# Pair stage: the second-layer products of two rounds issued in one stretch

## What is computed

```python
h = jnp.einsum('bsd,fd->bsf', xn, W1)                                   # 128 features
pair = jax.nn.relu(h[:, :, None, :] - h[:, None, :, :] + b1)
pair = jax.nn.relu(jnp.einsum('bijf,gf->bijg', pair, W2) + b2)          # first product, 128 -> 64
sim = jnp.einsum('bijg,og->bijo', pair, W3)[..., 0] + b3[0]             # second product, 64 -> 1
sim = sim.at[:, diag, diag].set(0.0)
_, top_idx = jax.lax.top_k(sim, 51)
```

## Time and profile before

| | |
|---|---|
| median of 3 runs | 3355.33 us (3354.02 to 3365.64) |
| the profiled execution | 3371.59 us, span 3370.1 us |
| pair stage in the span | 43.7 to 1131 us |
| attention a after it, to | about 1690 us |
| feed-forward, attention b, feed-forward | the rest |
| mean granted TensorE clock | 0.963 of full speed |
| PE / DVE / ACT busy over the span | 93% / 63% / 45% |

### The profile page before, as it was taken

How to read it: one execution, slowest core, us unless ns; L and a number is a source line. 1 busy time by engine, 2 the same in 40 slices (tenths; PEclk the granted TensorE clock), 3 DMA queues, 4 the chain that set the end, 5 groups by cost and what they waited for, 6 DMA issues and landing times.

```text
span 3370.1 us, 44081 instructions
## 1 busy us (share of the span) xinstructions
PE 3147.4 (93%) x17024; PEld 1740.1 (52%) x17041; DVE 2132.8 (63%) x4098; ACT 1518.2 (45%) x2512; POOL 572.6 (17%) x423
## 2 busy tenths in 40 slices
PE   6999999999999799999889999987898987999999
PEld 2333333333333344444268888853444434888887
DVE  5887988888888777667154434444766765443443
ACT  4877877777787356666521111112433442111110
POOL 0000000000000533343010100002543551001100
PEclk9999999999999799999889999988999998999999
DMA  2000000000000000000010100014323311000001
GB/s 70 1 1 11 1 1 11 1 1 11 1 1 1 1 1 1 2 1 1 1 75 19 38 19 1 1 61 115 93 65 88 97 36 75 19 19 19 19 1 50
DMA packets 32245, 86.94 MB, mean 26 GB/s; under 512 B 7139, under 2 KB 7140, under 8 KB 29605
## 3 DMA queue, kind: packets, MB, share of 16 engines
q1 hardware_dynamic: 29702, 83.96, 8.4%
q10 hardware_dynamic: 2336, 0.17, 0.0%
HBM read 59.60 MB, written 20.97 MB: 24 GB/s over the span
## 4 chain that ended last, share of the span: by engine, by line
PE 40%; DVE 3%; POOL 2%; issue 2%; DMA 2%; ACT 1%; SPq 0%; POOLq 0%; DVEq 0%; ACTq 0%
PE ps L1113 21%; PE ps L1127 10%; PE ps L1472 3%; POOL ex_sum L1440 2%; PE ps L1536 2%; PE ps L1503 1%; PE ps L1460 1%; PE ps L1514 1%; PE ps L1488 1%; DMA k_stack<-halves 1%; DMA halves<-lo_b 0%; PE ps L1525 0%; DMA ffn_raw<-in_w_ffn 0%; PE ps L1095 0%; DVE ffn_z L1139 0%
## 5 line engine op out<-in xcount | busy, mean ns | idle before, releaser
L626 DVE TENSOR_SCALAR pair_in<-key_words,row_words 128x512 f32<-128x512 f32 x1792 | 727.0, 480 | 75.9 <-PE ps L513 72.9
L711 ACT ACTIVATE pair_mid<-ps,row_bias 128x512 f32<-128x512 f32 x896 | 573.6, 686 | 236.9 <-PE ps L513 192.4
L513 PE MATMUL ps<-pair_in,w_hi 128*64 128x512 f16 x3584 | 610.4, 393 | 26.5 <-DVE pair_in L626 25.5
L1191 ACT ACTIVATE ffn_silu<-ps 128x512 f32<-128x512 f32 x128 | 76.4, 597 | 829.6 <-PE ps L1113 829.6
L1154 DVE TENSOR_TENSOR ffn_inner<-ffn_silu,ps 128x512 f32<-128x512 f32 x128 | 87.9, 687 | 566.5 <-PE ps L1113 566.5
L513 PEld LDWEIGHTS ps<-pair_in,w_hi 128*64 128x64 f16 x3584 | 204.5, 108 | 403.5 <-ACT pair_mid L711 189.1
L923 DVE TENSOR_REDUCE maxes<-ps 128x2 f32<-128x1024 f32 x256 | 307.8, 1224 | 129.5 <-PE ps L858 127.0
L966 ACT ACTIVATE ex<-ps 128x512 f32<-128x512 f32 x512 | 294.1, 597 | 149.1 <-PE ps L877 132.5
L513 PE MATMUL ps<-pair_in,w_lo 128*64 128x512 f16 x1792 | 354.0, 389 | 0.0
L1113 PE MATMUL ps<-ffn_z_hi,ffn_w_hi 128*128 128x512 f32 x1024 | 276.9, 392 | 7.6 <-DVE ffn_z_lo L1146 7.6
L1113 PE MATMUL ps<-ffn_z_lo,ffn_w_hi 128*128 128x512 f32 x1024 | 276.2, 392 | 0.0
(11 more groups left out here) (190 smaller groups left out, 4164.1 us busy)
## 6 DMA issues: line engine op xcount, KB each, us to landing
ffn_raw<-in_w_ffn SPq DMA_DIRECT2D x16, 1536.0 KB, 6.7
q_stack<-halves SPq DMA_DIRECT2D x48, 256.0 KB, 5.1
k_stack<-halves SPq DMA_DIRECT2D x48, 256.0 KB, 5.9
halves<-hi_b SPq DMA_DIRECT2D x16, 512.0 KB, 2.6
halves<-lo_b SPq DMA_DIRECT2D x16, 512.0 KB, 3.6
x<-in_x SPq DMA_DIRECT2D x8, 512.0 KB, 5.5
out<-x SPq DMA_DIRECT2D x4, 1024.0 KB, 4.3
wb_qk<-in_wb_qk SPq DMA_DIRECT2D x1, 2048.0 KB, 8.3
```

Of the source, the lines that this page charges most:

```text
L513: s = nc.tensor.matmul(ps[F2 * half:F2 * half + F2, bank + which, :], w_part[:, :], words.rearrange("p (s two) -> p s two", two=2)[:, :, o ...
L626: s = nc.vector.tensor_scalar(p.pair_in[:, (4 * n + i) % N_PAIR, :], p.key_words[:, b % 2, :], p.row_words[:, b % 2, row:row + 1], None, A ...
L711: nc.scalar.activation(p.pair_mid[:, n % NG, which, :], ps[:, bank + which, :], ACT.Relu, bias=bias).then_inc(p.mid_made, 1)
```

## The change

`layer2` steps are collected: the list `behind` takes every round, and only behind `pair` of an odd round are all the collected ones issued, those of the round two back and of the round before. Behind `pair` of an even round nothing is issued. `sim` of a tile comes with `layer2` of its round 15, so it now stands behind `pair` and `act_row` of round 1 of the next tile, and is followed by `layer2` of that tile's round 0. The ring `pair_mid` has 8 groups in place of 4 (16 KB more in each partition). No instruction is added or removed. DVE's own order is the same as before.

```diff
-N_PAIR, NG = 16, 4
+N_PAIR, NG = 16, 8
...
-    rounds, behind = [], None
+    rounds, behind = [], []
...
             if r % 2 and (tile, r) != (B * NT - 1, 15):
                 order.append(("act_row", tile + (r + 2) // 16, (r + 2) % 16))
-            if behind:
-                order.append(("layer2", *behind))
-                if behind[1] == 15:
-                    order.append(("sim", behind[0]))
-                    rounds += [("top", behind[0], i) for i in range(8)]
-            behind = (tile, r)
+            if r % 2:
+                for step in behind:
+                    order.append(("layer2", *step))
+                    if step[1] == 15:
+                        order.append(("sim", step[0]))
+                        rounds += [("top", step[0], i) for i in range(8)]
+                behind = []
+            behind.append((tile, r))
             if r % 2 and rounds:
                 order.append(rounds.pop(0))
...
-    order += [("layer2", *behind), ("sim", behind[0])]
+    order += [("layer2", *step) for step in behind] + [("sim", B * NT - 1)]
```

## The result

The changed kernel takes 3433.34 us (median of 6 runs, 3427.9 to 3446.11) against 3359.4 us of the kernel before in the same runs: ratio 1.0224, 95% interval 1.0202 to 1.0246. The forecast was 3426, 71 us above the median it was made on; measured are 74.

What follows compares the result with a forecast made beforehand. PE was taken to bound the pair stage. Double rounds 0, steps behind even rounds -2, late scores 58.9 and clock 14 sum to +71 us on the 3355.3 median: 3426 us, range 3388 to 3450.

Steps and rivals of the forecast that it cites:

- The change of tile shape: PE, plain double round: `layer2` moved beside the other avoids switching from 64-wide to 32-wide tiles and back, saving 0.26 us.
- The bank wait: PE, plain double round: third group waits for ACT to empty the first group's PSUM banks, costing 0.26 us.
- The late scores: Tile ends: later `sim` delays DVE, so PE stands 4.38 us more in 12 tiles, 2.1 in three: 58.9 us.
- L: Start of `layer2` of round 15 at a tile's end; `sim` forecast 2.55 us after it, PE's restart 7.39 after.
- The clock: Twelve long PE waits at tile ends: clock falls in all, ten more than now, at 1.4 us each: 14 us.
- The bound of 2.9 per fall: Upper bound on clock loss at tile ends: 2.9 us in all twelve places, 35 less the 3 paid now.
- The steps behind even rounds: 15 places with a projection step behind an even round: 0.13 us saved each, the bank wait hidden, -2 us.
- the full saving: Rival: ACT's copies don't hold PE in double rounds, 33 us saved beside the tile-end loss; 3395 or 3385 us; chance 0.13.
- no saving: Rival: second `layer2` drains the array too, 33 us more, 3459 us; chance 0.05.
- the heavier clock: Rival: clock falls at tile-end waits cost 32 us, 3444 us in all; chance 0.13, shared with ACT falling behind.
- Faster: Rival: 33 us saved in double rounds and late `sim` covered, 3322 us; gains below 2.2 us a tile; chance 0.04.

Runs made afterwards that it cites:

- e3: Changed kernel, but PE signals each PSUM bank when full, and ACT and PE wait bank by bank: 3389.23 us, ratio 1.0098.
- e6: Changed kernel with DVE's first look at the scores one odd round later and PSUM banks signalled one by one: 3301.91 us, ratio 0.983.
- e1: Changed kernel, but behind round 0 of each tile the last tile's round 15 `layer2` and `sim` are issued at once: 3355.78 us, ratio 0.9988.
- e8: Changed kernel, but the two `layer2` steps stand behind the even round in place of the odd: 3365.37 us, ratio 1.0021.
- e2: Changed kernel, but in round 1 of a tile ACT's `sim` goes ahead of its two rows (`act_row`): 3409.77 us, ratio 1.0155.
- e5: Changed kernel, but DVE's looks at a tile's scores (`top`) each stand one odd round later: 3321.36 us, ratio 0.9898.
- e4: Changed kernel, but PE issues 22 pairs of filler fp16 products before round 2's first group, reaching eleven waits: 3418.8 us, ratio 1.0183.
- e7: Kernel before, unpaired, with `top` one odd round later and PSUM banks signalled one by one: 3327.4 us, ratio 0.991.

## Why the forecast was right

- **The change of tile shape, -0.26 a double round.** Right: e3 and e6 show 7.84 become 7.58 to 7.60.
- **The bank wait, +0.26.** Right: 0.46 between the slots as forecast, the net is nothing to 0.01 (7.84), and e3 removes it by letting ACT start earlier. The price rests on the one place in the trace of before where two rounds followed each other: it gave the 0.05 from ACT's end to PE's start, which holds here too. Its own wait was only 0.18. The prediction puts the wait down to the reading of PSUM as the limit; e3 narrows this, since the same copies hold PE up no more once ACT starts on a bank as soon as it is full.
- **The late scores, 58.9 us.** Right in place and size: L + 2.55 and L + 7.39 to the hundredth. PE's wait for DVE grew by 58.2. e1 and e8 show that it is the place of round 15's `layer2` and of `sim` that costs, e2 that 1.2 of the 4.4 is ACT's queue, e5 that it is a wait of DVE at the wrong point of its own order.
- **The clock, 14 us.** Right in kind, 4 us short in size. Twelve falls in place of two, as assumed; but ten of them last 6.8 us and not the 3.4 of the earlier trace rows. The excess over 4.38 in the twelve places is 70.9 - 52.6 = 18.3 us; 14 were forecast. In e4 eleven places without a fall are 20.7 us shorter, 1.9 each and not 1.4. This is more than the excess over the kernel before, since that one had paid 2.8 for its own two falls. The bound of 2.9 per fall was not reached: 0.7 to 3.1 us of each fall lie in PE's wait. That all twelve waits would bring a fall was an assumption, since only two of the six waits in the trace of before had one; it came true.
- **The steps behind even rounds, -2 us.** Right in size by and large: nine of these double rounds are 0.13 to 0.15 shorter, as reckoned, and five 0.25 to 0.53. The -2.8 of all others together holds more that the forecast didn't have: the stage's first double round is 0.9 shorter, and four are 0.3 longer.

The sum, 71 us, was short by the clock's 4; the rest of the distance between 3426 and 3433 is the median of before, which over more runs is 3359 to 3361 and not 3355. Of the rivals, the full saving fell because the bank wait is there (it needs e3's edit), no saving fell with 7.58, and the heavier clock asked for 32 us, where 18 were measured. Faster needed a price under 2.2 us for a tile; it was 77 / 15 = 5.1.

## What to carry to other kernels

When steps are gathered to save a change of tile shape, look for what hangs on the last of them: here a quarter of a microsecond in each double round would have been 2.1 us a tile, and one late hand-over in sixteen rounds, to an engine whose own order hadn't changed, cost 5.1. A step that is taken out from between others may have been the time in which another engine caught up: reckon the ring (here two pairs of banks) without it, and signal its halves one by one if they are needed one by one. Let a consumer ask for a result only when it is surely there; moving the question back one step was worth more (33 us off the kernel before, by the medians of e7, whose bank signals leave the plain double round at 7.84) than the pairing (25 us). The pairing is only worth something with both: with the bank signals alone (e3) the kernel is slower than before, with the later question alone (e5) the stage is as long as the unpaired one. And count the places that an edit really reaches: e4 was written for twelve and reached eleven, and the twelfth, left as it was, shows what the filler does.

## What was not expected of the hardware

The length of PE's wait alone doesn't say how long the granted clock stays at 1.2 GHz. In the kernel before, six waits of 2.5 to 2.7 us brought two falls of 3.4 us. In e8, three waits of 3.3 us brought one of 3.4 us each, and three of 3.5 us none. In e2, six waits of 4.25 us brought 3.4 us each; in e3, six of 4.8 us brought 6.8 us each. In the changed kernel, six waits of 5.47 us brought 6.8 us in four places and 3.4 us in two, and all that were longer brought 6.8 us. With filler work for 5 us of the wait, in eleven places of e4, there was no fall; in the one place of that run without it, the wait of 5.47 us brought 6.8 us (the 0.62 of 1126 to 1135 is the mean over that fall). What decides between 3.4 and 6.8 us was not found, and no run was made for it.
